# A graph layer and an LSTM on one core: the stores of the gate inputs move from the sync engine into GpSimd's gather queue

## The chip, the core and the metric

The kernel runs on 1 core of one Trainium2 chip. The metric is the device time of one execution in microseconds, and it was taken without the profiler: 1757.74 us, the median of 2 runs (1756.25 and 1759.24).

In the rows, PE is TensorE (PEld its weight loads), DVE is VectorE, ACT is ScalarE, POOL is GpSimd and SP is the sync engine. SPq and POOLq are the sequencers of these engines, which issue DMAs.

## What is computed

`x` has 6250 rows of 256 numbers. A layer norm, a linear layer and a sum over 100,000 weighted edges make the first half; an LSTM with 256 hidden units over the 6250 rows, with a readout that needs sums before and behind each row, makes the second half. The reference, cut to what matters:

```python
support = jnp.einsum('ni,oi->no', layernorm(x), W_weight) + W_bias
messages = support[col] * edge_weight[:, None]          # 100,000 gathered rows
x = x + jax.ops.segment_sum(messages, row, num_segments=6250)

x_proj = einsum('btd,gd->btg', layernorm(x), W_ih) + b_ih + b_hh     # "gate inputs", 1024 per row
def step(carry, xp):
    gates = xp + h @ W_hh.T
    i, f, g, o = jnp.split(gates, 4, axis=-1)
    c = sigmoid(f) * c + sigmoid(i) * tanh(g)
    h = sigmoid(o) * tanh(c)
...
w = g * lstm_out                                          # g is 0 or 1, from two logits
x = x + 2.0 * lstm_out + (cumsum(w) - w) * fw_att + (total(w) - cumsum(w)) * bw_att
```

## The kernel before

**How the LSTM is made parallel.** The 6250 rows are cut into 125 segments of 50 rows (`SEGS`, `SEGL`). A step handles one place of all 125 segments at once. Each segment warms up over 64 steps (`WARM`) from a zero state on the rows ahead of it and then runs its own 50 steps. That makes 114 steps. The gate inputs of a place, 128 partitions by 1016 numbers (508 KB), are wanted more than once: in the step that follows their making, and again in later steps. So each place's gate inputs are stored once to the DRAM scratch `gate_input_scratch` (`xp_d`) and loaded from there 64 times.

**How the edges are summed.** The kernel sorts the edges into 881 tiles of 128 edges. For each tile POOL issues one gather (an indirect DMA) of 128 rows of 1 KB from `support_scratch` into a slot of `ring` (in `big_a`). PE multiplies the tile with a one-hot matrix and DVE adds the product to `x` in `big_b`. Tiles 0 to 244 are the first portion. Tiles 245 to 880 (636 tiles, the second portion) are taken by place.

**The stage around the change.** The second portion runs in 53 halves (`HALVES`) of 12 tiles (`PACE`), numbered h = 0 to 52. The ring has 24 slots, 12 for even halves and 12 for odd ones. In each half, function `place` of every engine runs once:

- ACT, `place` (L707): it waits until PE has done the tiles of half h-1, then copies the row numbers for the gathers of half h+1 (L618, semaphore `gst`). Then `take_input` (L656) takes the gate inputs of place u = h-4 from PSUM into `pr`, one of two buffers (L662), and signals `xe_r[0]` and `xe_r[1]`. From the third place on it first waits on `st2`: the store of place u-2 out of the same buffer must have landed (L660).
- PE, `place` (L1664): 12 tiles (L1616) with, between them, the projection of the place's gate inputs (L1635) and the product with `h` (L1642), then a transpose (L1624).
- POOL, `gather_place` (L533): it waits on `gst`, then issues 12 gathers (L538). It has no other work in this stage.
- SP, `store_gate_input` (L412): for each place j it waits on `xe_r[1]` and issues the store (L415). It has no other work in this stage.

So the gate inputs of place j are ready within half j+4. LAG is 3 and says how far the places run behind the tiles.

**Behind the stage.** After the last half SP loads gate inputs again (`load_gate_input`, L424). The loads for steps 50 and 51 wait for 24 stores of each buffer, the loads from step 52 on for all 50. POOL goes on with `output` (L548), the sums of the readout.

What paces POOL in the stage:

```python
def gather_place(it, q):
    pool.wait_ge(gst, it * 2 + (halves[0] + q + 1))
    pool.sem_inc(go, 1)
    for n in range(PACE):
        ...
```

Of the kernel before, what the change touches and what calls it, by code (L numbers as in the profile page):

```python
# [12 lines left out]
SEGS, SEGL = 125, 50  # L13
# [27 lines left out]
FIFTIETH, FRACTION = 5243, 18  # L41
LEAD = WARM - SEGL
LAG = 3
XW = SEGS + 2
XC = 8 * XW
TOL = 2.0 ** -19
# [6 lines left out]
HALVES = TIL[1] // PACE  # L53
# [5 lines left out]
def build(nc, A, out, slow_sweeps=SEGS, tol=TOL):  # L59
# [6 lines left out]
    ds = bass.ds  # L66
# [4 lines left out]
    xp_d = nc.dram_tensor("gate_input_scratch", [SEGL, P, XC], f32).ap()  # L71

    with ExitStack() as ctx:
        def sb(name, shape, dt=f32):
            return ctx.enter_context(nc.sbuf_tensor(name, shape, dt))
# [4 lines left out]
        def sem(name):  # L80
            return ctx.enter_context(nc.semaphore(name))
# [53 lines left out]
        pr = sb("pr", [P, 2, G4])  # L135
# [11 lines left out]
        def at(home, first, rows, *dims, dt=f32):  # L147
            size = 1
            for n in dims:
                size *= n  # L150
            words = -(-size // 2) if dt == bf16 else size
            view = home[0:rows, first:first + words]
            if dt != f32:
                view = view.bitcast(dt)[:, 0:size]
            names = "abcde"[:len(dims)]
            spaced = " ".join(names)
            return view.rearrange(f"p ({spaced}) -> p {spaced}", **dict(zip(names, dims))) if len(dims) > 1 else view
# [59 lines left out]
        x1 = big_b[0:SEGS, :, :]  # L217
        taken_in = [at(flat_c, 8192 + 1024 * q, P, 8, XW) for q in range(2)]
        gate_in = [pr[:, q, 0:XC].rearrange("p (c k) -> p c k", c=8) for q in range(2)]
# [70 lines left out]
        xe_r = [sem(f"gate_input_ready{x}") for x in range(2)]  # L290
        st2 = [sem(f"gate_input_stored{i}") for i in range(2)]
# [59 lines left out]
        def _(sp):  # L351
# [35 lines left out]
            for g in range(-(-NB // STORED)):  # L387
                first, n = g * STORED, min(STORED, NB - g * STORED)
# [20 lines left out]
                sp.dma_start(tile[:, :, :], A[name].rearrange("(k p) f -> p k f", p=P)).then_inc(load_w, 16)  # L409
            load_records(1)  # L410

            def store_gate_input(j, l, q):  # L412
                sp.wait_ge(xe_r[1], j + 1)
                row = l if isinstance(l, int) else sp.snap(l)
                sp.dma_start(xp_d[ds(row, 1), :, :].rearrange("o p n -> p (o n)"), pr[:, q, 0:XC]).then_inc(st2[q], 16)  # L415

            with sp.Fori(0, LEAD // 2) as it:
                for q in range(2):
                    store_gate_input(it * 2 + q, it * 2 + (SEGL - LEAD + q), q)
            with sp.Fori(LEAD // 2, SEGL // 2 - 1) as it:  # L420
                for q in range(2):
                    store_gate_input(it * 2 + q, it * 2 + (q - LEAD), q)

            def load_gate_input(u, l, q):  # L424
                if not isinstance(u, int) or u >= SEGL + 2:
                    for x in range(2):
                        sp.wait_ge(seeded[x], u - 1)
                row = l if isinstance(l, int) else sp.snap(l)
                sp.dma_start(taken_in[q].rearrange("p c k -> p (c k)"), xp_d[ds(row, 1), :, :].rearrange("o p n -> p (o n)")).then_inc(xp_l[q], 16)

            for q in range(2):
                sp.wait_ge(st2[q], 16 * (SEGL // 2 - 1))
                load_gate_input(SEGL + q, SEGL - LEAD + q, q)
            for q in range(2):
                store_gate_input(SEGL - 2 + q, SEGL - 2 + q - LEAD, q)
            for q in range(2):
                sp.wait_ge(st2[q], 16 * (SEGL // 2))
            with sp.Fori(SEGL // 2 + 1, WARM // 2) as it:
# [6 lines left out]
            def store_result(nth):  # L445
                for i, (first, end) in enumerate(zip(LEAVING, LEAVING[1:])):
                    sp.wait_ge(res, nth * (len(LEAVING) - 1) + i + 1)
                    for a, b in PARTS:
                        sp.dma_start(out.rearrange("(k l) f -> k l f", l=SEGL)[a:b, first:end, :],
                                     own[a:b, first:end, :]).then_inc(out_s, 16)  # L450
# [2 lines left out]
            sp.wait_ge(flg, 1)  # L453
            ok = sp.value_load(flag[0:1, 0:1], min_val=0, max_val=1)
            with sp.If(ok == 0):
                with sp.Fori(0, SEGL // 2) as it:
                    for q in range(2):
                        store_gate_input(it * 2 + (SEGL + q), it * 2 + q, q)
                for q in range(2):
                    sp.wait_ge(st2[q], 16 * SEGL)  # L460
                with sp.Fori(0, slow_sweeps) as sweep:
                    with sp.Fori(0, SEGL // 2) as it:
                        for q in range(2):
                            load_gate_input(sweep * SEGL + it * 2 + (STEPS + q), it * 2 + q, q)
                store_result(1)
                sp.wait_ge(out_s, STORES * 2)
                sp.sem_inc(sgo, 1)
# [3 lines left out]
        def _(pool):  # L471
# [61 lines left out]
# [4 lines that stand above are left out]
                    s = q * PACE + n  # L537
                    pool.indirect_dma_start(  # L538
                        out=ring[:, s, :], out_offset=None, in_=sup_d,
                        in_offset=bass.IndirectOffsetOnAxis(ap=stg_g[:, q, n:n + 1], axis=0)).then_inc(gat2[s], 16)  # L540

            with pool.Fori(0, HALVES // 2) as it:
                for q in range(2):
                    gather_place(it, q)
            gather_place(HALVES // 2, 0)


            def output(j, n, q):  # L548
                w = weighed[q]
                pool.wait_ge(terms_r, n + 1)  # L550
                if not isinstance(n, int) or n > 0:
                    pool.wait_ge(o_v, n)
                G.tensor_tensor(t_s, run, diff, ALU.mult)  # L553
                G.tensor_tensor(t_o, w, bw[0:SEGS, :], ALU.mult).then_inc(step_t, 1)
                pool.wait_ge(step_t, n + 1)
                G.tensor_tensor(run, run, w, ALU.add).then_inc(run_s, 1)
                G.tensor_tensor(t_s, t_s, t_o, ALU.subtract).then_inc(step_s, 1)
                pool.wait_ge(step_s, n + 1)
                mine = own[:, ds(j, 1), :].rearrange("k l f -> k (l f)")
                G.tensor_tensor(mine, mine, t_s, ALU.add).then_inc(o_v, 1)  # L560
# [10 lines left out]
            pool.wait_ge(flg, 1)  # L571
            ok = pool.value_load(flag[0:1, 0:1], min_val=0, max_val=1)
            with pool.If(ok == 0):
                with pool.Fori(0, slow_sweeps) as sweep:
                    with pool.Fori(0, SEGL // 2) as it:
                        for q in range(2):
                            output(it * 2 + q, sweep * SEGL + it * 2 + (SEGL + q), q)

        @block.scalar
        def _(act):  # L580
# [36 lines left out]
            def stage_gather(tile0, q, count=HALF):  # L617
                nc.scalar.copy(stg_g[:, q, 0:count], row_of[:, ds(tile0, count)]).then_inc(gst, 1)  # L618
# [37 lines left out]
            def take_input(j, q, x, free=None):  # L656
# [4 lines left out]
                for c in range(4):  # L661
                    ins = nc.scalar.activation(gate_in[q][:, 4 * x + c, 2:XW], bank[2 + x][:, c * SEGS:(c + 1) * SEGS],  # L662
                                               ACT.Identity, bias=bias[:, 4 * x + c:4 * x + c + 1])
                ins.then_inc(xe_r[x], 1)

            def copy_input(j, q, first=False):
                copy_transposed(j, q, xt_p2, pj2[1], xt_r2, first, 2)
# [21 lines left out]
            def tanh_c(u, q, x):  # L689
                act.wait_ge(c_r[x], u + 1)  # L690
                nc.scalar.activation(act_c[:, x, :], c_s[:, 1 - q, x, :], ACT.Tanh).then_inc(a_c[x], 1)  # L691
# [7 lines left out]
            def take_and_seed(u, q, w):  # L699
                for x in range(2):  # L700
                    take_input(u, q, x, None if isinstance(u, int) and u < 2 else u - 1)
                    act.wait_ge(xe_r[x], u + 1)
                    if not isinstance(u, int) or u > 0:
                        act.wait_ge(a_o[x], u)
                    seed_half(q, x, w, 0, gate_in)

            def place(it, q, w=0, last=False):  # L707
                h = 2 * it + q if isinstance(it, int) else HALVES
                j, u = it * 2 + (q - LAG), it * 2 + (q - LAG - 1)
                if h > LAG + 1:  # L710
                    tanh_c(u - 1, 1 - q, 1)
                if h > 0 and not last:
                    act.wait_ge(prod, it * WIDE + (RING + TFROM[1] + q * PACE))
                    stage_gather(it * WIDE + (TFROM[1] + (q + 1) * PACE), 1 - q, PACE)
                if h > LAG:
                    take_and_seed(u, q, w)
                    for x in range(2):
                        gates(u, q, x, False, 0)
                    tanh_c(u, q, 0)
                if h >= LAG:  # L720
                    copy_input(j, 1 - q, h < LAG + 2)

# [6 lines left out]
            act.wait_ge(bits, 1)  # L729
            for it in range(LAG):  # L730
                for q in range(2):
# [1102 lines left out]
```

## Time and profile before

| what | value |
|---|---|
| time without the profiler, median of 2 runs | 1757.74 us |
| the profiled execution, from its first to its last instruction | 2362.0 us |
| PE busy in it | 1644.3 us (70%) |
| DVE busy in it | 1357.8 us (57%) |
| POOL busy in it | 1166.9 us (49%) |
| ACT busy in it | 532.0 us (23%) |
| gathers of the second portion (L538) | 636, 949 ns each |
| stores of the gate inputs (L415) | 50, 508 KB each |

The profiled execution is 604 us longer than a run without the profiler. Each time of a row below is one of the profiled execution. A row of the timeline gives the start, the duration, the engine, the line, the operation and, in brackets, how long the engine had been idle before it and who released it. "issue" stands where the engine waited for nothing that the profile shows.

### The profile page before, as it was taken

How to read it: one execution, taken by the hardware profiler on the slowest of the kernel's cores; microseconds unless marked ns; L12 is line 12 of the kernel's file. 1: busy time of each engine (PE TensorE's matmuls, PEld its weight loads, DVE VectorE, ACT ScalarE, POOL GpSimd, SP SyncE). 2: the span in 40 equal slices, each digit the busy share in tenths (PEclk: the TensorE clock that was granted, in tenths of full speed). 3: DMA queues.
4: the chain of work that ended last, by engine and by line, in shares of the span. 5: the costliest groups of instructions: out<-in, count | busy, mean ns of one | idle time of the engine just before them, and what ended most of it. 6: DMA issues, size and time to landing. Idle time of an engine off the chain costs nothing.

```text
span 2362.0 us, 35522 instructions
## 1 busy us (share of the span) xinstructions
PE 1644.3 (70%) x9417; PEld 1363.5 (58%) x9417; DVE 1357.8 (57%) x4075; ACT 532.0 (23%) x1838; POOL 1166.9 (49%) x1235
## 2 busy tenths in 40 slices
PE   5696766666664576576676676676776776889994
PEld 3385555555552365465565565565565555889993
DVE  8997787777763444344444444444443444556666
ACT  1121000000000022222221222221222222566662
POOL 0377556556545535444444444444344354027774
PEclk9898787878885778777777777787787777999997
DMA  6112222322222223223223223223232233233334
GB/s 169 35 43 61 72 73 68 99 71 73 71 64 80 80 81 93 84 71 95 82 76 95 78 78 94 76 84 93 71 93 84 71 94 101 89 115 114 113 113 131
DMA packets 71694, 202.43 MB, mean 86 GB/s; under 512 B 22785, under 2 KB 25046, under 8 KB 70773
## 3 DMA queue, kind: packets, MB, share of 16 engines
q0 software_dynamic: 48048, 116.84, 18.1%
q1 hardware_dynamic: 23600, 85.04, 11.1%
q8 instruction: 20, 0.33, 0.1%
q14 instruction: 26, 0.21, 0.0%
HBM read 160.49 MB, written 41.17 MB: 85 GB/s over the span
## 4 chain that ended last, share of the span: by engine, by line
PE 45%; issue 20%; DVE 20%; another core or an unknown queue 8%; DVEq 3%; ACT 3%; DMA 0%; POOL 0%; SPq 0%; ACTq 0%
PE bank L1642 14%; PE bank L1616 13%; PE bank L1635 7%; PE bank L1573 5%; PE bank L1540 3%; DVE big_a L999 3%; DVE big_b L1054 2%; DVE big_a L995 2%; DVEq L1057 2%; PE bank L1624 1%; DVE big_c L1048 1%; DVE big_c L997 1%; DVE listed L938 1%; DVE w_ih L938 1%
## 5 line engine op out<-in xcount | busy, mean ns | idle before, releaser
L538 POOL DMA_INDIRECT big_a<-support_scratch,stg_g x636 | 603.8, 949 | 692.2 <-ACT stg_g L618 513.8
L1054 DVE TENSOR_TENSOR big_b<-big_b,bank 125x256 f32 x881 | 367.1, 417 | 663.3 <-remote 396.6
L1642 PE MATMUL bank<-big_c 128*128 128x125 f32 x3648 | 520.8, 287 | 290.7 <-issue 247.9
L1642 PEld LDWEIGHTS bank<-big_c 128*128 128x128 f32 x3648 | 481.2, 199 | 325.4 <-issue 292.2
L1616 PE MATMUL bank<-big_a,big_c 128*125 128x256 f32 x1272 | 474.4, 479 | 122.6 <-issue 94.8
L1616 PEld LDWEIGHTS bank<-big_a,big_c 128*125 128x125 f32 x1272 | 258.6, 239 | 206.8 <-issue 182.4
L1048 DVE TENSOR_SCALAR big_c<-consts_sb,listed 128x125 f32<-128x125 f32 x881 | 308.2, 351 | 76.8 <-issue 49.5
L511 POOL DMA_INDIRECT big_a<-support_scratch,stg_g x245 | 233.9, 955 | 185.3 <-ACT stg_g L618 117.1
L1573 PE MATMUL bank<-big_a,big_c 128*125 128x256 f32 x490 | 171.9, 481 | 151.7 <-issue 91.1
L1635 PEld LDWEIGHTS bank<-xt,w_ih 128*128 128x128 f32 x1600 | 234.6, 213 | 26.0 <-ACT xt L592 10.3
L1635 PE MATMUL bank<-xt,w_ih 128*128 128x125 f32 x1600 | 235.9, 296 | 1.0 <-ACT xt L592 0.8
L1540 PEld LDWEIGHTS bank<-big_a,big_c 125*128 125x128 f32 x1600 | 212.2, 215 | 22.7 <-DVE big_a L999 14.7
L1540 PE MATMUL bank<-big_a,big_c 125*128 125x128 f32 x1600 | 211.3, 297 | 14.9 <-DVE big_a L999 11.6
L1573 PEld LDWEIGHTS bank<-big_a,big_c 128*125 128x125 f32 x490 | 98.8, 227 | 210.8 <-issue 175.1
L684 ACT ACTIVATE big_c<-bank 128x250 f32<-128x250 f32 x128 | 48.9, 382 | 574.2 <-remote 555.3
L662 ACT ACTIVATE pr<-bank,gate_bias 128x125 f32<-128x125 f32 x400 | 113.3, 366 | 147.2 <-remote 106.5
L691 ACT ACTIVATE big_c<-big_c 128x125 f32<-128x125 f32 x228 | 70.3, 308 | 289.9 <-DVE big_c L1201 289.9
L618 ACT CAST stg_g<-listed 128x12 uint32 (+4 forms) x84 | 15.8, 190 | 441.0 <-PE bank L1573 316.3
L553 POOL TENSOR_TENSOR listed<-listed 125x256 f32<-125x256 f32 x50 | 36.3, 727 | 142.1 <-DVE listed L1330 142.0
L491 POOL TENSOR_TENSOR pr<-pr,b_gnn 125x256 f32<-125x256 f32 x50 | 75.0, 1518 | 31.2 <-ACT pr L603 30.5
L997 DVE TENSOR_TENSOR big_c<-bank,consts_sb 125x2560 f32<-125x2560 f32 x30 | 84.4, 2815 | 0.0
L999 DVE TENSOR_TENSOR big_a<-big_a,bank 125x2560 f32<-125x2560 f32 x30 | 84.3, 2810 | 0.0
(238 smaller groups left out, 1695.0 us busy)
## 6 DMA issues: line engine op xcount, KB each, us to landing
big_c<-gate_input_scratch SPq DMA_DIRECT2D x64, 508.0 KB
gate_input_scratch<-pr SPq DMA_DIRECT2D x50, 508.0 KB
big_a<-support_scratch,stg_g POOLq DMA_INDIRECT x881
support_scratch<-pr SPq DMA_DIRECT2D x12, 448.0 KB
big_b<-in_x SPq DMA_DIRECT2D x2, 1904.0 KB
out<-big_a SPq DMA_DIRECT2D x2, 1456.0 KB
big_b<-in_x SPq DMA_DIRECT2D x1, 1792.0 KB
out<-big_a SPq DMA_DIRECT2D x1, 1344.0 KB
```

The lines of the kernel that those rows point to most:

```text
L511: pool.indirect_dma_start(out=ring[:, s, :], out_offset=None, in_=sup_d, in_offset=bass.IndirectOffsetOnAxis(ap=stg_g[:, q, j:j + 1], axis ...
L538: pool.indirect_dma_start(out=ring[:, s, :], out_offset=None, in_=sup_d, in_offset=bass.IndirectOffsetOnAxis(ap=stg_g[:, q, n:n + 1], axis ...
L662: ins = nc.scalar.activation(gate_in[q][:, 4 * x + c, 2:XW], bank[2 + x][:, c * SEGS:(c + 1) * SEGS], ACT.Identity, bias=bias[:, 4 * x + c ...
L997: V.tensor_tensor(slot_h[:, q], s.broadcast_to([EP, CC, P]), several(iota[0:EP, :], CC), ALU.is_equal)
L999: V.tensor_tensor(col_v[:, q], col_h.rearrange("p c (o n) -> p c o n", o=1).broadcast_to([EP, CC, 2, NPOS]), given[:, 0:2, :].rearrange("p ...
L1048: V.tensor_scalar(oneh[:, s % HOTS, 0:SEGS], iota[:, 0:SEGS], src_of[:, ds(t, 1)], w_of[:, ds(t, 1)], ALU.is_equal, ALU.mult).then_inc(oh_ ...
L1054: V.tensor_tensor(at, at, bank[4 + s % PSR][0:SEGS, 0:D], ALU.add).then_inc(added, 1)
L1540: ins = mm(bank[b][:, 0:2 * NPOS], slot_h[:, q, c, :], col_v[:, q, c, :, :].rearrange("p v n -> p (v n)"), start=q == 0 and c == 0, stop=q ...
L1573: mm(bank[4 + s % PSR][0:SEGS, 0:D], oneh[:, s % HOTS, 0:SEGS], ring[:, s % RING, :], start=True, stop=True).then_inc(prod, 1)
L1616: mm(bank[4 + s % PSR][0:SEGS, 0:D], oneh[:, s % HOTS, 0:SEGS], ring[:, s, :], start=True, stop=True).then_inc(prod, 1)
L1635: ins = mm(bank[2 + x][:, c * SEGS:(c + 1) * SEGS], w_ih[:, k, g:g + P], xt[:, q, k, 0:SEGS], start=k == 0, stop=k == 1)
L1642: return mm(bank[b + x][:, c * SEGS:(c + 1) * SEGS], w_hh[:, k, g:g + P], h_s[:, q, k, :], start=False, stop=True, skip_group_check=True)
```

## The change

GpSimd now issues the stores of the gate inputs in the second portion, and SP issues none. The new function `store_behind(j, l, q)` has the same three lines as `store_gate_input` had: the wait for `xe_r[1]`, the row, the DMA with its signal to `st2[q]`. It stands ahead of the gathers of half h, for place j = h-6 (`BEHIND` is LAG+3). The first store stands ahead of half 6. The store of place 46 stands ahead of the last half's gathers (h = 52), and those of places 47, 48 and 49 stand behind them. In the branch that runs only when the warm-up was too short (it isn't taken with these inputs) the stores move in the same way.

```diff
+BEHIND = LAG + 3
...
-            def store_gate_input(j, l, q):
-                sp.wait_ge(xe_r[1], j + 1)
-                row = l if isinstance(l, int) else sp.snap(l)
-                sp.dma_start(xp_d[ds(row, 1), :, :].rearrange("o p n -> p (o n)"), pr[:, q, 0:XC]).then_inc(st2[q], 16)
...
-            with sp.Fori(LEAD // 2, SEGL // 2 - 1) as it:
-                for q in range(2):
-                    store_gate_input(it * 2 + q, it * 2 + (q - LEAD), q)
...
             for q in range(2):
-                store_gate_input(SEGL - 2 + q, SEGL - 2 + q - LEAD, q)
-            for q in range(2):
                 sp.wait_ge(st2[q], 16 * (SEGL // 2))
...
-            with pool.Fori(0, HALVES // 2) as it:
+            def store_behind(j, l, q):
+                pool.wait_ge(xe_r[1], j + 1)
+                row = l if isinstance(l, int) else pool.snap(l)
+                pool.dma_start(xp_d[ds(row, 1), :, :].rearrange("o p n -> p (o n)"), pr[:, q, 0:XC]).then_inc(st2[q], 16)
+
+            begun_storing, turned_over = BEHIND // 2, (BEHIND + LEAD) // 2
+            with pool.Fori(0, begun_storing) as it:
                 for q in range(2):
                     gather_place(it, q)
+            with pool.Fori(begun_storing, turned_over) as it:
+                for q in range(2):
+                    store_behind(it * 2 + (q - BEHIND), it * 2 + (q - BEHIND + SEGL - LEAD), q)
+                    gather_place(it, q)
+            with pool.Fori(turned_over, HALVES // 2) as it:
+                for q in range(2):
+                    store_behind(it * 2 + (q - BEHIND), it * 2 + (q - BEHIND - LEAD), q)
+                    gather_place(it, q)
+            store_behind(HALVES - 1 - BEHIND, HALVES - 1 - BEHIND - LEAD, 0)
             gather_place(HALVES // 2, 0)
+            for j in range(HALVES - BEHIND, SEGL):
+                store_behind(j, j - LEAD, j % 2)
```

This is what POOL's program holds in the loop of the second portion before the change, two halves to one turn (`gather_rows_staged` is the semaphore `gst`):

```order
L538 DMA big_a<-support_scratch,stg_g 128x256 [waits gather_rows_staged]
L538 DMA big_a<-support_scratch,stg_g 128x256 x11
L534 REGISTER_ALU
L538 DMA big_a<-support_scratch,stg_g 128x256 [waits gather_rows_staged]
L538 DMA big_a<-support_scratch,stg_g 128x256 x11
L542 REGISTER_ALU
```

And this is the end of POOL's loop after the change, with what follows it up to the readout (`gate_input_ready1` is the semaphore `xe_r[1]`; L522 is the gather, L529 the store):

```order
L529 ISA [waits gate_input_ready1]
L529 DMA gate_input_scratch<-pr 128x1016
L518 REGISTER_ALU
L522 DMA big_a<-support_scratch,stg_g 128x256 [waits gather_rows_staged]
L522 DMA big_a<-support_scratch,stg_g 128x256 x11
L539 REGISTER_ALU
L539 COMPARE_AND_BRANCH
L529 DMA gate_input_scratch<-pr 128x1016 [waits gate_input_ready1]
L522 DMA big_a<-support_scratch,stg_g 128x256 [waits gather_rows_staged]
L522 DMA big_a<-support_scratch,stg_g 128x256 x11
L529 DMA gate_input_scratch<-pr 128x1016 [waits gate_input_ready1] x3
```

One store with its wait now stands ahead of each set of 12 gathers, and three stand behind the last set.

On SP the program after the change goes straight from the loads of the records to the loads of the gate inputs (L418); before, two loops and two single instructions with stores stood between and around them:

```order
L402 DMA big_a<-record_scratch 128x3x256
L404 DMA big_a<-record_scratch 124x256
L418 DMA big_c<-gate_input_scratch 128x1016 [waits gate_input_stored0]
L418 DMA big_c<-gate_input_scratch 128x1016 [waits gate_input_stored1]
L425 UNCONDITIONAL_BRANCH [waits gate_input_stored1,gate_input_stored0]
```

SP has nothing left to do while the second portion runs.

## Rows read from the trace of the kernel before

**Rows 1.** The page: the span, busy times and the POOL gathers' group.

```profile
span 2362.0 us, 35522 instructions
PE 1644.3 (70%) x9417; PEld 1363.5 (58%) x9417; DVE 1357.8 (57%) x4075; ACT 532.0 (23%) x1838; POOL 1166.9 (49%) x1235
L538 POOL DMA_INDIRECT big_a<-support_scratch,stg_g x636 | 603.8, 949 | 692.2 <-ACT stg_g L618 513.8
```

**Rows 2.** Busy time by stage (us; count), granted clock, DMA share, GB/s.

```profile
core 0: us, PE busy (x) PEld busy (x) DVE busy (x) ACT busy (x) POOL busy (x), PEclk, DMA share, GB/s
713.00:2028.00 1315.00, 880.60 (x4542) 719.62 (x4542) 583.54 (x2476) 284.31 (x993) 603.76 (x636) 0.76 0.28 84
835.00:1335.00 500.00, 341.02 (x1798) 282.80 (x1798) 222.49 (x961) 114.36 (x400) 227.79 (x240) 0.77 0.28 84
1219.00:1222.00 3.00, 2.58 (x12) 1.98 (x12) 0.53 (x4) 0.00 (x0) 2.39 (x3) 0.60 0.86 270
1219.80:1221.50 1.70, 1.65 (x6) 1.14 (x5) 0.05 (x1) 0.00 (x0) 1.18 (x2) 0.50 1.07 381
```

**Rows 3.** Waits of POOL: who for whom, us in total, times, longest.

```profile
POOL big_a L538 <- ACT stg_g L618: 513.8, 51, 12.9
POOL big_a L538 <- issue: 178.4, 585, 0.3
POOL big_a L511 <- ACT stg_g L618: 117.1, 27, 8.5
```

**Rows 4.** Timeline of POOL: one half's 12 gathers and the next's first.

```profile
1211.26 0.95 POOL L538 DMA_INDIRECT big_a<-support_scratch,stg_g  x1 [10.05 <-ACT stg_g L618]
1212.51 0.95 POOL L538 DMA_INDIRECT big_a<-support_scratch,stg_g  x1 [0.30 <-issue]
...
1225.03 0.95 POOL L538 DMA_INDIRECT big_a<-support_scratch,stg_g  x1 [0.31 <-issue]
1236.38 0.95 POOL L538 DMA_INDIRECT big_a<-support_scratch,stg_g  x1 [10.40 <-ACT stg_g L618]
```

**Rows 5.** Timeline of PE: a stretch at its pace, and one behind it.

```profile
1211.90 0.60 PE L1616 MATMUL bank<-big_a,big_c 128*125 128x256 f32 x2
1212.34 1.05 PE L1635 MATMUL bank<-xt,w_ih 128*128 128x125 f32 x8
1213.22 1.03 PE L1616 MATMUL bank<-big_a,big_c 128*125 128x256 f32 x4
1214.09 1.05 PE L1642 MATMUL bank<-big_c 128*128 128x125 f32 x8
...
1222.66 0.37 PE L1642 MATMUL bank<-big_c 128*128 128x125 f32 x1 [1.04 <-issue]
1224.10 0.37 PE L1642 MATMUL bank<-big_c 128*128 128x125 f32 x1 [1.07 <-issue]
```

**Rows 6.** Timeline of ACT: transposes of the last two halves, after the last gather.

```profile
2009.32 0.35 ACT L592 COPY xt<-bank 128x250 f32<-128x250 f32 x1
2023.09 0.35 ACT L592 COPY xt<-bank 128x250 f32<-128x250 f32 x1
```

**Rows 7.** Timeline of POOL: the second portion's first waits, and its last gather.

```profile
770.50 0.95 POOL L538 DMA_INDIRECT big_a<-support_scratch,stg_g  x1 [11.32 <-ACT stg_g L618]
809.20 0.94 POOL L538 DMA_INDIRECT big_a<-support_scratch,stg_g  x1 [8.82 <-ACT stg_g L618]
...
2002.21 0.94 POOL L538 DMA_INDIRECT big_a<-support_scratch,stg_g  x1 [0.30 <-issue]
```

**Rows 8.** Durations on their lines (min/median/max in ns), the store and the record scatter.

```profile
L415 SPq DMA_DIRECT2D gate_input_scratch<-pr x50: 332/332/373, 826.9 to 2028.5; - x50
L538 POOL DMA_INDIRECT big_a<-support_scratch,stg_g x636: 942/949/1084, 714.1 to 2002.2; - x159
L482 POOL DMA_INDIRECT record_scratch<-stg_r,stg_i x30: 1544/1582/1622, 273.1 to 699.3; - x30
```

**Rows 9.** Timeline of ACT: gate inputs taken (L662), next row numbers copied (L618).

```profile
1216.99 1.13 ACT L662 ACTIVATE pr<-bank,gate_bias 128x125 f32<-128x125 f32 x4 [4.31 <-remote]
1235.41 0.18 ACT L618 CAST stg_g<-listed 128x12 uint32 x1
1236.71 0.58 ACT L670 COPY bank<-pr 128x500 f32<-128x500 f32 x1
```

**Rows 10.** Timeline of SP at the end of the stage.

```profile
1996.91 0.33 SPq L415 DMA_DIRECT2D gate_input_scratch<-pr  x1
1997.72 2.83 SPq L429 DMA_DIRECT2D big_c<-gate_input_scratch  x2
```

## What the change should do to the time

> **What bounds the kernel now.** I read four things in this order: the busy times and the span, the busy time by stage, POOL's waits, and then the timeline of one half of the second portion.
>
> The first thing to see is that the profiled execution isn't the one that is timed. Its span is 2362.0 us [rows 1], the median without the profiler is 1757.7 us. So 604 us of the span are gone in a plain run, and the question is where. The stage that the change touches lasts 1315 us of the span and has 53 halves, 24.8 us each; in its steady part 240 gathers, that is 20 halves, take 500 us, 25.0 us each [rows 2].
>
> In such a half POOL issues 12 gathers, one each 1.25 us (0.95 us and 0.30 us to the next), 15.0 us in all, and then waits about 10 us for ACT's next row numbers [rows 4]. Over the stage these waits sum up to 513.8 us, and in the first portion the same waits sum up to 117.1 us [rows 3]. PE alternates between two paces. At its own pace one tile and eight matmuls take 1213.22 - 1211.90 = 1.32 us, and two tiles alone take 1214.09 - 1213.22 = 0.87 us. Later in the same half, single matmuls come only every 1.4 us, and the profile names nothing that they wait for ("issue") [rows 5]. A half has 12 tiles and 64 of the matmuls in eights, so at PE's own pace it needs 8 x 1.32 + 4 x 0.44 = 12.3 us. Where no gather is in flight any more, after the last one at 2002.21 [rows 7], the last two halves show how fast the whole loop through PE, ACT and DVE can turn: 2023.09 - 2009.32 = 13.8 us [rows 6].
>
> I take from this: PE, ACT and DVE can turn a half in 12.3 to 13.8 us, POOL needs 15.0 us. The 10 us of waiting for ACT in the profile are there because all the others are slowed down while the gathers run. In a plain run 604 us are missing, and POOL's own 15.0 us per half are the last thing that I'd expect to shrink, since the gathers take 942 to 949 ns from minimum to median [rows 8]. The waits of POOL for ACT are 513.8 + 117.1 = 630.9 us, about what is missing. So in a plain run **POOL's issue of gathers is the bound of the stage**, with nearly no wait left: at least 630.9 - 604.3 = 26.6 us. Of these the first two waits of the second portion, 11.3 + 8.8 = 20.1 us [rows 7], come before any store can be in POOL's queue. That leaves about 6.5 us.
>
> **What it removes.** SP no longer issues 50 stores of 0.33 us [rows 8]. SP has nothing else to do in this stage, nobody waits for its sequencer, so that is worth nothing.
>
> **What it adds.** POOL issues 47 stores between sets of gathers (places 0 to 46) and 3 behind the last gather. The trace shows no direct store issued by POOL. Its cost is bounded by the nearest rows: below by SP's 0.33 us for the same store, above by POOL's scatter of the records, 1.58 us, with 0.30 us to the next 1.88 us [rows 8]. It is nearest to a gather: the same engine, 128 rows on the SBUF side, no addition. I take the gather's 0.95 + 0.30 = 1.25 us. In the profiled execution this goes into a wait of 10 us per half and costs nothing, so the span there should stay at 2362 us within its spread. In a plain run nothing covers it: 47 x 1.25 = 58.8 us, less the 6.5 us of waits that may be left, is 52 us. 1757.7 + 52 = **1810 us**, and POOL's half grows from 15.0 to 16.3 us. The three last stores have only the readout's sums behind them on POOL, which don't begin until later.
>
> **The waits that it adds.** The store of place h-6 waits for `xe_r[1]`, with all gathers of half h queued behind it, and PE waits for these. Is that wait ever the last? The gate inputs of that place are finished by ACT in its half h-2, the row numbers for half h are copied at the start of ACT's half h-1, so always later. In the profile the inputs are ready at 1216.99 + 1.13 = 1218.1 and the row numbers at 1235.4, 17 us behind [rows 9]. POOL's gathers end at 1226.0 in between [rows 4], so the wait costs nothing. The other way round, ACT waits for the store of place u-2 before it overwrites the buffer. That store now leaves POOL ahead of the gathers of half u+4, while ACT wants it in its own half u+4. That is most of a half, over 10 us, and the transfer takes about 2 us. I cost it at nothing; if that cover were gone, it would cost up to the transfer, 47 x 1.4 = 64 us.
>
> **The end of the stage.** SP's loads for steps 50 and 51 wait for the stores of places 46 and 47. SP had stored at 1996.91 and loaded at 1997.72 [rows 10]; POOL is busy with gathers until 2003.2 [rows 7], so these loads come some 7 us later. ACT wants them behind the last place, after the transpose of 2023.09 [rows 6], so 20 us cover 7.
>
> **A rule weighed against the rows.** The transfer itself, 508 KB at 381 GB/s, lasts about 1.4 us and takes all 16 DMA engines: their share is 1.07 [rows 2]. It has the same bytes on whichever queue. The Trainium skill (DMA: Bandwidth & Descriptors, section "Issuing engines are not separate DMA queues") says that transfers run on the same 16 engines whoever starts them, so that another issuing engine only saves sequencer time, which is usually small. By that rule the change would be worth nothing in the transfer and a small loss on POOL. The rows agree on the first; on the second they decide how small: 1.25 us on an engine that has none to spare.
>
> **The rivals.**
>
> *The store hides (chance 0.30).* If POOL's gather is cheaper without the profiler, for example if the 0.30 us between two belongs to the profiler, a half's gathers take 12 x 0.95 = 11.4 us and a store makes it 12.3 us, below the 13.8 us of the loop [rows 4, 6]. Then nothing changes: 1757.7 us. Against it: the stage would then lose 53 x (24.8 - 13.8) = 583 us, and the first portion's stalls come on top, which together is more than the 604 us by some tens. For it: only one of the two paces has to be off by 10%.
>
> *The store is dearer than a gather (chance 0.08).* At the scatter's 1.88 us it is 47 x 1.88 = 88 us less 6.5: 1840 us. The Trainium skill (SBUF — State Buffer, the box on the "DVE blocks DMA" trap) says that GpSimd can't write its descriptors while DVE holds the shared ports in some modes, and gives 3.1 us in place of 0.62 us. The gathers here run beside the same DVE work and spread by only 0.14 us from minimum to maximum [rows 8], so this trace doesn't show it.
>
> *Faster (chance 0.06).* Before, SP's store starts in the middle of the gathers and fills the DMA engines for 1.7 us [rows 2]; after, it starts at the head of a set. If PE waits for landings and not POOL for its own issue, each half gives back the transfer, 1.4 us: 47 x 1.4 = 64 us, 1694 us. It decides from the point where a gather's landing, and not its issue, is what PE waits for in a plain run. Against it: POOL issues the gathers beside the store at the same 1.25 us, and the bytes of the store still lie ahead of the next 12 gathers.
>
> **How the numbers follow.** POOL-bound with a store like a gather has 0.56, and its own range is 1790 us (half of the cost covered by waits that I don't see) to 1822 us. With the rivals' 0.30 at 1757, 0.08 at 1840 and 0.06 at 1694, the range that leaves out no more than 2 in 10 is 1752 to 1838 us. About 2%, here 35 us, is what a measurement of this kernel can tell from no change; the line is at 1793 us. Slower: 0.56 and 0.08, less 0.03 for the low end of the first, 0.61. Same: 0.30 and 0.03, 0.33. Faster: 0.06.
>
> **What would show it.** In the profile of the changed kernel: 50 direct DMAs on POOL with about 0.95 us each; if they take 0.3 or 1.6 us, the sum scales with it. POOL's waits for ACT shrink from 10.0 to about 8.8 us per half, and the span stays. The stores start right behind the twelfth gather, with no wait for `xe_r[1]`; a wait there that is the last before a gather would prove the argument on the waits wrong. And the loop of 13.8 us should be seen again behind the last gather. The whole forecast fails if the plain run has POOL waiting 1.25 us or more per half, which no profile shows directly; it takes runs with POOL's work made longer or shorter.

## The result, and the profile after

The changed kernel takes 1788.43 us (median of 2 runs, 1788.08 to 1788.79) against 1757.74 us: 30.7 us more, a ratio of 1.0168 with a 95% interval of 1.0151 to 1.0184. It is slower, by 1.7%.

The page of the changed kernel differs from [rows 1] by far more than 30 us. Its first lines, and its group of the second portion's gathers:

```profile
span 1786.4 us, 35468 instructions
PE 1461.0 (82%) x9417; PEld 1243.2 (70%) x9417; DVE 1368.9 (77%) x4075; ACT 539.7 (30%) x1838; POOL 1203.6 (67%) x1285
...
L522 POOL DMA_INDIRECT big_a<-support_scratch,stg_g x636 | 609.5, 958 | 200.9 <-issue 188.9
```

The span is 1786.4 us, which fits the times. The span of 2362.0 us in [rows 1] doesn't fit the times of its own kernel. The prediction put the difference down to the profiler. That was wrong, as the first experiment shows: a second profile of the same kernel has a span of 1758.0 us. The sets of runs below fall into two kinds: in three the unchanged kernel has a median of 2348 to 2370 us, in two, and in the times of before, one of 1758 to 1761 us. By its span the page of before is of the slow kind. Each set was taken on a chip of its own, so the text speaks of slow and fast chips; whether the chip is the reason, or something else that differed between the sets, isn't shown. So the page of after is not to be compared with it, but with the second profile of the kernel before, below.

One set of gathers with the store behind it, in the timeline of GpSimd of the changed kernel:

```profile
1015.45 0.95 POOL L522 DMA_INDIRECT big_a<-support_scratch,stg_g  x1 [0.30 <-issue]
1016.70 0.94 POOL L522 DMA_INDIRECT big_a<-support_scratch,stg_g  x1 [0.30 <-issue]
1017.95 0.95 POOL L522 DMA_INDIRECT big_a<-support_scratch,stg_g  x1 [0.30 <-issue]
1018.89 0.59 POOL L529 DMA_DIRECT2D gate_input_scratch<-pr  x1
1019.78 0.97 POOL L522 DMA_INDIRECT big_a<-support_scratch,stg_g  x1 [0.30 <-issue]
```

The store starts at once when the gather ends and takes 0.59 us; the next gather follows 0.30 us behind it. From gather to gather it is 1019.78 - 1017.95 = 1.83 us with a store between them and 1.25 us without one. A store costs 0.58 us there.

### The profile page after: what moved, and what is told of

It is laid out like the page before. It is cut to its first block, busy times and chain, and to the rows that moved or that the text cites. A ratio compares the mean times of both kernels' runs of the same rounds, so it can differ in the third digit from the quotient of the medians.

```text
span 1786.4 us, 35468 instructions
## 1 busy us (share of the span) xinstructions
PE 1461.0 (82%) x9417; PEld 1243.2 (70%) x9417; DVE 1368.9 (77%) x4075; ACT 539.7 (30%) x1838; POOL 1203.6 (67%) x1285
## 4 chain that ended last, share of the span: by engine, by line
PE 31%; DVE 23%; POOL 22%; issue 16%; ACT 3%; DMA 2%; DVEq 1%; POOLq 0%; ACTq 0%; SPq 0%
POOL big_a L522 21%; PE bank L1646 12%; PE bank L1577 6%; PE bank L1544 5%; PE bank L1620 5%; DVE big_a L1003 5%; PE bank L1639 3%; DMA big_a<-support_scratch,stg_g 2%; DVE big_a L999 2%; DVE big_c L1205 1%; DVE big_c L1001 1%; DVE listed L942 1%; DVE w_ih L942 1%; ACT big_c L695 1%; POOL gate_input_scratch L529 1%
## 5 line engine op out<-in xcount | busy, mean ns | idle before, releaser
L522 POOL DMA_INDIRECT big_a<-support_scratch,stg_g x636 | 609.5, 958 | 200.9 <-issue 188.9
L1620 PE MATMUL bank<-big_a,big_c 128*125 128x256 f32 x1272 | 415.8, 416 | 108.1 <-issue 58.3
L1646 PEld LDWEIGHTS bank<-big_c 128*128 128x128 f32 x3648 | 445.9, 191 | 46.0 <-issue 35.4
L1646 PE MATMUL bank<-big_c 128*128 128x125 f32 x3648 | 456.5, 277 | 24.6 <-DVE big_c L1210 24.6
L1052 DVE TENSOR_SCALAR big_c<-consts_sb,listed 128x125 f32<-128x125 f32 x881 | 323.4, 368 | 71.9 <-PE bank L1620 56.1
L1620 PEld LDWEIGHTS bank<-big_a,big_c 128*125 128x125 f32 x1272 | 202.8, 199 | 191.6 <-DVE big_c L1052 86.4
L1639 PEld LDWEIGHTS bank<-xt,w_ih 128*128 128x128 f32 x1600 | 222.1, 201 | 13.9 <-ACT xt L596 1.0
L1577 PE MATMUL bank<-big_a,big_c 128*125 128x256 f32 x490 | 153.7, 453 | 84.6 <-DVE big_b L1058 72.7
L1639 PE MATMUL bank<-xt,w_ih 128*128 128x125 f32 x1600 | 221.1, 284 | 0.8 <-ACT xt L596 0.8
L1544 PEld LDWEIGHTS bank<-big_a,big_c 125*128 125x128 f32 x1600 | 198.3, 203 | 19.6 <-DVE big_a L1003 16.2
L1544 PE MATMUL bank<-big_a,big_c 125*128 125x128 f32 x1600 | 198.4, 286 | 12.9 <-DVE big_a L1003 12.9
L1577 PEld LDWEIGHTS bank<-big_a,big_c 128*125 128x125 f32 x490 | 96.9, 218 | 130.1 <-DVE big_c L1052 84.3
```

The lines of the kernel that those rows point to most:

```text
L522: pool.indirect_dma_start(out=ring[:, s, :], out_offset=None, in_=sup_d, in_offset=bass.IndirectOffsetOnAxis(ap=stg_g[:, q, n:n + 1], axis ...
L1052: V.tensor_scalar(oneh[:, s % HOTS, 0:SEGS], iota[:, 0:SEGS], src_of[:, ds(t, 1)], w_of[:, ds(t, 1)], ALU.is_equal, ALU.mult).then_inc(oh_ ...
L1544: ins = mm(bank[b][:, 0:2 * NPOS], slot_h[:, q, c, :], col_v[:, q, c, :, :].rearrange("p v n -> p (v n)"), start=q == 0 and c == 0, stop=q ...
L1577: mm(bank[4 + s % PSR][0:SEGS, 0:D], oneh[:, s % HOTS, 0:SEGS], ring[:, s % RING, :], start=True, stop=True).then_inc(prod, 1)
L1620: mm(bank[4 + s % PSR][0:SEGS, 0:D], oneh[:, s % HOTS, 0:SEGS], ring[:, s, :], start=True, stop=True).then_inc(prod, 1)
L1639: ins = mm(bank[2 + x][:, c * SEGS:(c + 1) * SEGS], w_ih[:, k, g:g + P], xt[:, q, k, 0:SEGS], start=k == 0, stop=k == 1)
```

## The experiments

Theory 1: GpSimd's issue of DMAs bounds the second portion, and a store costs what its issue takes there. The rivals: the loop through TensorE, ScalarE and VectorE bounds it; the bytes of the store in the gathers' queue, and not its issue, cost the time; ScalarE's wait for the store costs it.

### The kernel before, profiled again

No edit.

> The kernel before, unchanged, for a second profile of it. The first one had a span of 2362 us against times of 1756 to 1759 us, the changed kernel's has 1786.4 us. Theory 1 (GpSimd's issue of the gathers bounds the second portion): the span is 1755 to 1760 us, the 10 us waits of GpSimd for the row numbers are gone (under 30 us in all over the second portion, where the first profile had 513.8 us), and twelve gathers follow one another without a gap, 15.0 to 15.2 us to a half. Rival (the loop through TensorE, ScalarE and VectorE bounds it): GpSimd waits 1 us or more in every half, over 50 us in all.

It took 1759.79 us, beside runs of the same kernel on that chip at 1758.17 us. The page's span, GpSimd's waits, and its gathers on their line:

```profile
span 1758.0 us, 35522 instructions
...
POOL big_a L538 <- issue: 191.6, 629, 0.3
...
POOL big_a L538 <- ACT stg_g L618: 9.2, 7, 7.3
...
L538 POOL DMA_INDIRECT big_a<-support_scratch,stg_g x636: 940/946/1346, 613.3 to 1414.4; - x159
```

GpSimd waits for ScalarE's row numbers 9.2 us in the whole second portion, 7 times, where [rows 3] has 513.8 us and 51 times. The first gather starts at 613.3 and the last at 1414.4: 801.1 us for 53 halves, 15.1 us each. In the changed kernel the same stretch is:

```profile
L522 POOL DMA_INDIRECT big_a<-support_scratch,stg_g x636: 942/949/1154, 613.5 to 1443.4; - x159
```

That is 829.9 us, 28.8 us more. What lies ahead of it is 0.2 us longer (613.5 against 613.3), and what lies behind it as long (1786.4 - 1443.4 = 343.0 us against 1758.0 - 1414.4 = 343.6 us). So the 28.4 us between the two spans all lie in the stage that the change touches, and the 47 stores between gathers, at 0.58 us, make 27.3 us of them. The first and the second profile also tell where the 604 us of the first profile lie: 100.8 us ahead of its first gather (714.1 against 613.3 us), 487.0 us from its first gather to its last (1288.1 against 801.1 us) and 16.2 us behind (359.8 against 343.6 us). The chain that ended last, in the second profile of the kernel before, shows the same bound:

```profile
PE 29%; DVE 24%; POOL 23%; issue 17%; ACT 3%; DVEq 2%; DMA 1%; POOLq 0%; ACTq 0%; SPq 0%
POOL big_a L538 23%; PE bank L1642 10%; PE bank L1573 6%; PE bank L1616 5%; PE bank L1540 5%; DVE big_a L999 5%; DVE big_a L995 2%; PE bank L1635 2%; DVE big_b L1054 1%; DVE big_c L997 1%; DVE listed L938 1%; DVE w_ih L938 1%; ACT big_c L691 1%; DVE big_c L1048 1%; DVE big_c L1201 1%
```

GpSimd's gathers are 23% of the chain, more than any other line.

### 11 and 10 gathers in a half, SP's stores

```diff
-                for n in range(PACE):
+                for n in range(PACE - 1):            # and PACE - 2
...
-                pe.wait_ge(gat2[s], nth * 16)
+                g = min(s, s // PACE * PACE + (PACE - 2))    # and PACE - 3
+                pe.wait_ge(gat2[g], nth * 16)
...
-                mm(..., ring[:, s, :], start=True, stop=True
+                mm(..., ring[:, g, :], start=True, stop=True
```

> The kernel before with 11 gathers in each half of the second portion in place of 12; the twelfth tile takes the rows of the eleventh, so its gather is the part of the computation that is left out. TensorE, ScalarE and VectorE do the same work. Theory 1 (GpSimd's issue is the bound): 53 x 1.25 = 66 us less, 1691 us. Rival (the loop is the bound, GpSimd has slack): no change, 1757 us.

> The kernel before with 10 gathers in each half (the last two tiles take the rows of the tenth; their gathers are left out). Theory 1: GpSimd needs 12.5 us for a half and the loop of 13.8 us takes over, so it stops at about 53 x 1.25 = 66 us less, 1691 us, 0 to 10 us from the run with 11 gathers, not at 132 us less. If the loop can turn faster than 13.8 us: down to 1625 us. Rival (the loop is the bound already): 1757 us.

With 11 gathers: 1723.02 us, a ratio of 0.9802 (0.9786 to 0.9819), 35.2 us less. With 10: 1716.76 us, 0.9762 (0.9746 to 0.9778), 41.4 us less. The direction is that of theory 1: less work on GpSimd and the same on all others makes the kernel faster, and most of it, 35.2 of 41.4 us, comes with the first gather taken away. The size isn't: 35 us, not 66. The loop of the others comes in at less room than the 13.8 us of [rows 6] promised. In these runs it turns in about 14.2 us: from 612.3 to 1364.1 (751.8 us) for 53 halves with 10 gathers:

```profile
L538 POOL DMA_INDIRECT big_a<-support_scratch,stg_g x530: 940/946/1410, 612.3 to 1364.1; - x177
its engine sat idle before it (us, times) until:
  issue: 148.7, 482
  ACT stg_g L618: 105.7, 48
```

GpSimd now waits 105.7 us for ScalarE; it is no longer the bound.

### 10 gathers in a half, GpSimd's stores

The edit for 10 gathers, in the changed kernel.

> The changed kernel with 10 gathers in each half, the same gathers left out. Now GpSimd has room for the store. Theory 1 (a store costs GpSimd's issue time, 0.65 us each): the store hides, the time is that of the kernel before with 10 gathers, within 5 us, in place of the 31 us that the change costs with 12. Rival (the bytes of the store in the gathers' queue, or ScalarE's wait for the store, cost the time): the 31 us are there with 10 gathers too.

1677.99 us, a ratio of 0.9542 (0.9526 to 0.9557) to the kernel before. The store hides, as theory 1 has it. But it does more: with room on GpSimd, the change is not neutral, it is 38.8 us **faster** than its partner with SP's stores (1716.76 us). Neither theory 1 (within 5 us) nor its rivals had expected that. Where the partners differ, in the waits of each (10 gathers, SP's stores first, then GpSimd's):

```profile
DVE rstd L1168 <- issue: 102.8, 50, 2.5
```

```profile
DVE rstd L1172 <- issue: 69.3, 50, 2.2
```

This is the idle time of VectorE in the middle of each half, 33.5 us of the 38.8 us. L1168 is the first instruction behind the second register load of the tile table (L1057, `dve.reg_load`), on which the next accumulation depends. What happens there with SP's stores is in the timeline of the first of the two:

```profile
1005.45 0.42 DVE L1054 TENSOR_TENSOR big_b<-big_b,bank 125x256 f32 x1
1005.54 0.58 ACT L670 COPY bank<-pr 128x500 f32<-128x500 f32 x1
1005.68 0.33 SPq L415 DMA_DIRECT2D gate_input_scratch<-pr  x1
...
1007.95 0.15 DVE L1168 TENSOR_SCALAR rstd<-sums 125x1 int32<-125x1 int32 x1 [2.08 <-issue]
```

SP's store is issued at 1005.68, while VectorE's load runs, and VectorE idles 2.08 us. Of the 50 idle times before this instruction, 44 are over 1.6 us with SP's stores and 3 with GpSimd's; the smallest is 1.24 us in both. These three are the ones where GpSimd's own store comes beside the load, in the first halves that have a store:

```profile
700.63 0.58 POOL L529 DMA_DIRECT2D gate_input_scratch<-pr  x1
...
703.68 0.15 DVE L1172 TENSOR_SCALAR rstd<-sums 125x1 int32<-125x1 int32 x1 [2.21 <-issue]
```

So the queue that issues the store doesn't matter here, but the moment does: GpSimd's store leaves at the head of a set of gathers, in all other halves but the last more than 3 us before the idle begins. The loads themselves (min/median/max in ns), with 10 gathers and SP's stores, and in the changed kernel with 12:

```profile
L1057 DVEq TENSOR_LOAD <-table x137: 594/1408/2522, 232.9 to 1369.3; - x137
```

```profile
L1061 DVEq TENSOR_LOAD <-table x137: 595/1405/1428, 232.4 to 1440.7; - x137
```

In the changed kernel no load is longer than 1.43 us; beside SP's stores the longest takes 2.52 us. Each of the 44 loads over 1.6 us in the run with SP's stores has a store issued between 0.41 us before its start and 0.27 us after it. The second profile of the kernel before shows the other side: there SP's store is issued 0.52 us or more after the start of 39 loads, and none of these takes over 1.48 us. Theory 2 is that a store issued beside VectorE's register load makes the load longer. It was tested by a second store of SP and by moving the load (below).

### Extra stores on GpSimd, beside SP's

GpSimd issues 47 stores more, from constant data, at the places that the change uses. SP keeps its own. The run with a second store on SP and the one with split stores belong to the same set; their edits are told in what was expected of them.

```diff
+            def store_behind(j, l, q):
+                row = l if isinstance(l, int) else pool.snap(l)
+                pool.dma_start(dump_d[ds(row, 1), :, 0:16].rearrange("o p n -> p (o n)"), flat_w[:, 0:16]).then_inc(dumped, 16)
...
+                    store_behind(it * 2 + (q - 6), it * 2 + (q - 6), q)
                     gather_place(it, q)
```

> The kernel before, whose stores SP goes on issuing, and on top GpSimd issues 47 direct stores of 128 x 16 numbers (8 KB) from constant data into a scratch that nobody reads, at the places where the changed kernel has its stores. It separates the issue of a store on GpSimd from its bytes. Theory 1 (the change costs GpSimd's issue: 0.59 us on the changed kernel's trace and some 0.06 us around it, with no wait left in the kernel before): 47 x 0.65 = 31 us more, 1788 us. Rival (the 508 KB in the gathers' queue, ahead of the next 12 gathers, cost the 31 us): no more than 5 us, 1758 to 1763 us.

> As the run with thin extra stores, but each extra store on GpSimd carries 508 KB. Theory 1: 31 us more again, 1788 us, within 5 us of the thin ones. Rival (bytes in the gathers' queue cost too): 1.4 us for each, up to 66 us above the thin ones.

> The kernel before with each store on SP followed by a second one of 508 KB from constant data into a scratch that nobody reads. No work is added to GpSimd. With GpSimd's gathers cut to 10 a half, SP's stores made the loop 39 us slower than GpSimd's stores, and VectorE idled 103 us instead of 69 us before L1168, behind its register load of the tile table. Theory 2 (the burst on the hardware queue delays VectorE's register load by 0.7 us a half; the kernel before has 0.5 to 0.7 us of room under GpSimd's 15.0 us): the second burst uses up the room and a little shows, 0 to 30 us more, and VectorE's idle time before L1168 rises from 72 us to 100 us or above. Rival (bytes on the hardware queue cost nothing): 1758 us, and 72 us before L1168.

> The changed kernel with each store cut into two of 508 columns, each on semaphores of its own: twice the stores on GpSimd, the same bytes. Theory 1 (the number of stores counts): 47 x 0.65 = 31 us more than the changed kernel, 1819 us. Rival (the bytes count): 1788 to 1793 us.

These four ran on a chip on which every kernel took about 2370 us, the kernel before too (2370.45 us, 31 runs). The ratios to it: thin stores 0.9990 (0.9965 to 1.0014), full ones 0.9990 (0.9969 to 1.0011), a second store on SP 1.0005 (0.9983 to 1.0028), and the changed kernel with each store cut in two 0.9965 (0.9946 to 0.9984). None of them costs anything there, and the split stores of the changed kernel are 8.6 us faster than the kernel before. That bears out one statement of the prediction for such a chip: GpSimd's waits of 10 us a half cover the stores. The waits take them up. With the full extra stores and with the split ones:

```profile
POOL big_a L541 <- ACT stg_g L630: 486.0, 51, 13.0
```

```profile
POOL big_a L526 <- ACT stg_g L627: 447.2, 51, 11.3
```

Against the 513.8 us of [rows 3], 47 full stores between gathers take 28 us out of the wait, 47 thin ones 23 us (490.9 us) and 94 half ones 67 us: 0.5 to 0.7 us each. The run with no store added to GpSimd has 518.9 us, so 5 us between such sums mean nothing, and 64 times the bytes don't show.

The second store on SP was the test of theory 2. With it (first line), against the run with thin stores, whose SP issues one store a half (second line), VectorE's idle time behind the register load is:

```profile
DVE rstd L1172 <- issue: 120.4, 50, 3.8
DVE rstd L1180 <- issue: 97.3, 50, 2.7
```

With one store of SP and none of GpSimd, in the first profile of before, it is 97.0 us; with the split stores on GpSimd and none on SP, 67.3 us. The longest load takes 3.83 us with two stores of SP, 2.53 us with one (2.70 us beside the thin ones) and 1.42 us with none. So the stores do lengthen the load, as theory 2 has it; the total time didn't follow (1.0005), so on such a chip that idle time isn't what the kernel waits for, and the test says nothing on what it is worth elsewhere.

On the stores of GpSimd where it has no wait, these runs are silent. So the thin stores ran once more:

> The kernel with 47 thin extra stores on GpSimd once more, since in the first measurement every kernel of the call, the one before included, took 2370 us, with GpSimd waiting 10 us a half, which covers any store. Where the kernel before takes 1757 us, theory 1 (issue time on GpSimd) still expects 31 us more, 1788 us, and the rival (the bytes in the gathers' queue) no more than 5 us.

1785.09 us on a chip where the kernel before takes 1761.45 us: a ratio of 1.0130 (1.0113 to 1.0147), 23.6 us more. Here is the issue of a store in the timeline of GpSimd:

```profile
1016.04 0.95 POOL L541 DMA_INDIRECT big_a<-support_scratch,stg_g  x1 [0.30 <-issue]
1016.99 0.58 POOL L547 DMA_DIRECT2D dump_scratch<-w_ih  x1
1017.87 0.98 POOL L541 DMA_INDIRECT big_a<-support_scratch,stg_g  x1 [0.30 <-issue]
```

A store of 8 KB takes as long to issue as one of 508 KB, 0.58 us, and the time from gather to gather is the same 1.83 us. The gathers go from 612.1 to 1440.2, 828.1 us, 27.0 us longer than in the second profile of before. So the issue alone makes most of the change's 30.7 us, with 64 times fewer bytes and with SP's stores still in place. The rival of the bytes, which allowed the thin stores at most 5 us, is out as the main cause. Between 23.6 and 30.7 us lie 7 us that may belong to the bytes or to the difference between chips; in the profiles the two kernels' gathers differ by 1.8 us only (829.9 and 828.1 us), which speaks against the bytes.

### The register load moved away from the store

Both kernels with 10 gathers in a half, and VectorE loads all 12 numbers at the start of the half.

```diff
-                vals = blocks(first + TFROM[1], PACE // 2)
+                vals = blocks(first + TFROM[1], PACE // 2) + blocks(first + (TFROM[1] + PACE // 2), PACE // 2, PACE // 2)
...
-                vals = blocks(first + (TFROM[1] + PACE // 2), PACE // 2)
```

> The kernel before with 10 gathers in each half (the last two tiles take the rows of the tenth), and with VectorE's second register load of the tile table moved from the middle of a half to its start, beside the first, so that it no longer falls beside SP's store. Theory 2 (with slack on GpSimd, SP's store costs 39 us because it delays VectorE's load in the middle of the half): the time falls from 1717 us to within 8 us of the same kernel with GpSimd's stores. Rival (the store on SP's queue delays something else, for example the landing of gathers): the 39 us between the two placements stay.

> The changed kernel with 10 gathers in each half and the same early register load. It is the partner of the run with SP's stores. Theory 2: 1678 us or up to 60 us less (VectorE's idle of 1.4 us in the middle of the half goes), and within 8 us of the partner. Rival: 39 us below the partner.

> The kernel before with 10 gathers in each half and VectorE's second register load moved to the start of the half, once more, since in the first measurement the kernel before took 2355 us on that chip and both placements took 2261 us. Where the kernel before takes 1757 us: theory 2 (SP's store costs 39 us at 10 gathers because it delays VectorE's load in the middle of the half) expects 1678 us or less, no idle time left before L1168, and no load longer than 1.5 us beside a store. Rival (the store on SP's queue delays something else): no more than the 1.4 us a half that the load itself took is gained, and what the store costs stays: 1717 - 50 x 1.4 + the 34 us of the store = about 1700 us or above.

All three ran on chips on which the kernel before takes 2355.27 and 2347.66 us. The two placements took 2262.73 us (0.9610, 0.9592 to 0.9628) and 2260.42 us (0.9583, 0.9546 to 0.9620), and the repeat 2261.64 us (0.9640, 0.9597 to 0.9683). There is no idle time left before L1168, but the two placements are alike there, and whether they differ without this edit on such a chip wasn't measured. All three are also 86 to 95 us faster than the kernel before, and how much of that the early load gives, and how much the two gathers left out, wasn't measured either. So the test doesn't decide what the 38.8 us are made of. That a store lengthens the load is shown by the second store on SP; that this makes 33.5 us of the 38.8 us is read from the waits, and from the chain that ended last, in which VectorE's sequencer (DVEq, the loads among others) has 6% with SP's stores and 2% with GpSimd's. The other 5 us are open.

## Why the prediction was right, and where it was off

The forecast was 1810 us within 1752 to 1838 us, and slower. It came out as 1788.4 us. The direction and the mechanism are right, and the cost is 30.7 us where 52 us were forecast. The range is no strong test: it holds no change as well. The result lies under the prediction's own line of 1793 us between slower and same, and just under its own range for this mechanism, 1790 to 1822 us. (Half of the store's 58.8 us would have given 1787 us for its low end; and 47 x 1.4 is 66 us, not 64. Neither changes the forecast.)

**The bound: right.** In the second profile of the kernel before, GpSimd issues one gather each 1.25 us with 9.2 us of waits in the whole second portion, and 15.1 us to a half where the prediction had 15.0 us. The prediction had 6.5 us of waits left for the stores to fill; they filled none, since the changed kernel waits 11.9 us for the row numbers. Taking gathers away made the kernel faster; adding issues made it slower.

**How that was argued: half right.** The argument set the missing 604 us against 630.9 us of waits. What was left, at least 26.6 us, came out near the truth: 9.2 us for the second portion and 16.9 us for the first, 26.1 us in all. But its statement that the profiler stretches the span is wrong: the second profile has a span of 1758.0 us, and on slow chips the plain times are as long as the first profile. The conclusion was right and the reason given for it wrong. What the slow chips do in the stretch of the gathers, first profile against second:

```profile
714.10:2002.20 1288.10, 858.83 (x4408) 700.05 (x4409) 567.05 (x2408) 273.63 (x955) 602.82 (x635) 0.76 0.28 84
613.30:1414.40 801.10, 709.00 (x4480) 598.51 (x4481) 587.82 (x2451) 283.50 (x974) 607.66 (x636) 0.97 0.45 137
```

TensorE is busy longer at a lower granted clock (0.76 against 0.97), and VectorE, ScalarE and GpSimd are busy about as long (567, 274 and 603 us against 588, 284 and 608 us), so they idle more. Why is open.

**The price of a store: this term was mis-sized.** The prediction took a gather's 1.25 us from gather to gather. The trace shows 0.58 us: 0.59 us for the store, which starts with no gap behind the gather, and 0.30 us to the next gather, which was there before. The lower bound, SP's 0.33 us, was nearer to it than the value taken. With 0.58 us, and no waits to fill, the sum is 47 x 0.58 = 27 us, against 28.4 us between the spans and 30.7 us between the medians. The choice "nearest to a gather" is what failed. Why a gather takes 0.95 us and a store 0.59 us, no run here shows.

**What SP's stores cost before: wrong.** The prediction gave nothing for their removal. They are worth 39 us as soon as GpSimd has room (1716.8 against 1678.0 us), and that was the mechanism of the rival "faster" in outline, a burst on SP's queue in the middle of the half, though, as far as the traces tell, through VectorE's register load and not through the landing of gathers. In the kernel before it is hidden: the loop with SP's stores turns in 14.2 us, under GpSimd's 15.1 us. And at GpSimd's pace the store mostly comes too late in the load to lengthen it: 8 of the 50 idle times before L1168 are over 1.6 us in the second profile of before, and none in the changed kernel.

**The waits it adds: right.** GpSimd waits once for the gate inputs, 7.7 us, ahead of the last store (1453.3), which stands behind the last gather (1443.4), so it costs nothing:

```profile
L529 POOL DMA_DIRECT2D gate_input_scratch<-pr x50: 544/587/736, 703.9 to 1453.3; - x50
...
its engine sat idle before it (us, times) until:
  ACT pr L666: 7.7, 1
```

TensorE waits more for gathers to land, 23.8 us against 2.4 us in the second profile of before and 13.4 us with the thin stores, which a later GpSimd would explain; whether the bytes of the stores have a part in it isn't shown. There is no wait of ScalarE for a store in the list of waits, and the loads at the end of the stage cost nothing: the 343 us behind the last gather didn't grow.

**The rivals.** "The store hides" is what the runs on slow chips show, and those with 10 gathers. "Dearer than a gather" is out: 0.74 us at most. The trap that the prediction took from the Trainium skill (SBUF — State Buffer, the box on the "DVE blocks DMA" trap) isn't seen on any of the 50 stores, which take 0.54 to 0.74 us; no run here shows whether VectorE was in one of the modes that the page means.

**The loop's 13.8 us** of [rows 6] was measured on the last halves, when no gather ran. With 10 gathers and GpSimd's stores the halves take (1327.4 - 611.8) / 53 = 13.5 us:

```profile
L522 POOL DMA_INDIRECT big_a<-support_scratch,stg_g x530: 942/946/1407, 611.8 to 1327.4; - x177
```

None of the experiments gave a version that beats both kernels and computes all: SP's stores stay the better placement while GpSimd must issue 12 gathers in each half.

## What to carry to other kernels

Before work is moved to an engine, count that engine's issue time in the stage, gaps included, and not its share of the whole span: GpSimd is busy for 67% of the second profile, less than TensorE (82%) and VectorE (78%), and its issue is the bound of the stage. Compare a profile's span with the times before any of its waits is trusted: if they don't fit, the profile was taken in other conditions, and its waits are room that may not exist. Here 47 issues of 0.58 us cost 27 us on the engine that was the bound, and nothing where it had room. A store can also cost through the moment at which it is issued: look at what runs beside it.

## What the runs showed of the hardware

- The issue of a direct store on GpSimd takes 0.58 us for 8 KB and 0.59 us for 508 KB (medians), and it starts without the 0.30 us gap that stands ahead of the next gather (0.95 us).
- VectorE's register load of six table entries takes 1.4 us at the median, with VectorE idle 1.24 us or more of it; beside a store it takes up to 2.7 us if SP issues the store and up to 2.26 us if GpSimd does (each in one run), and none of the 137 loads of the changed kernel takes over 1.43 us. A second store beside it made it up to 3.83 us.
- The same kernel has medians of 1758 to 1761 us in some sets of runs and of 2348 to 2370 us in others, each set on a chip of its own. 487 of the 604 us lie in the stretch of the second portion's gathers, where the granted clock is 0.76 in place of 0.97 and VectorE and ScalarE idle more, while GpSimd's own issue keeps its 1.25 us. The cause wasn't found.
